# One projection of 40 rows for dt's low rank, B and C, with B and C repeated over the channels by transfers through DRAM

## The chip, the cores and the metric

The kernel runs on one core of one Trainium2 chip. The core has five engines that work side by side and meet only at semaphores: TensorE (PE in the profile; PEld is its loading of weights), VectorE (DVE), ScalarE (ACT), GpSimd (POOL) and SyncE (SP), and 16 DMA engines that all queues share. The metric is the device time of one launch in microseconds, lower is better, as a median over several runs.

## The reference, cut to what matters

Eight images of 48 x 48 tokens with 128 features pass three layers: a state space layer, a linear attention layer and a mixture of eight experts (top 2). The change lies in the first. For each token, with a 3x3 convolution `xc` of 256 channels, it computes

```python
xp = xc @ W_xproj                      # 256 -> 8 + 16 + 16
dt_r, Bp, Cp = xp[..., :8], xp[..., 8:24], xp[..., 24:]
dt  = softplus(dt_r @ W_dt + b_dt)     # 8 -> 256
dtN = dt @ W_dtN + b_dtN               # 256 -> 16
# scan over the 2304 tokens, state h of 256 channels x 16 states
h = exp(dt[:, :, None] * A) * h + (dtN * B)[:, None, :] * x[:, :, None]
y = einsum('bdn,bn->bd', h, C) + Dskip * x
```

and then a layer norm, a gate `silu(z)` and an output projection. `B` and `C` have 16 values for each token, the same for all 256 channels.

## The kernel before

An image is cut into NC = 6 chunks of T = 384 tokens. The scan puts (state n, channel j) pairs on the 128 partitions: 16 states times 8 channels make one block, so 32 blocks (NB) make a chunk, and one block is one *step*. A whole image is 192 steps, all eight images 1536. Each engine runs one long written-out program over steps k = 0 to 191 of a pass (`c, n = divmod(k, 32)`: chunk c, step n of the chunk). In one pass the scan of image i, the projections for the chunk after it, the convolution for the chunk after that, the attention of image i-1 (`w.j`, steps 22 to 125), and the experts of the two images before that (`w.p`, `w.q`; their tiles on steps 126 to 191 and 0 to 26) are interleaved by hand; the loop over passes is a pipeline of images. Nothing is scheduled at run time: an engine does its instructions in the written order and waits at each semaphore.

One step works like this. PE copies x to the 128 partitions with a small product (`spread`, L768, three PSUM banks, at most two steps ahead of the scan). DVE multiplies it in PSUM by `db_rep` (`inflow`, L1407) and scans (`scan`, L1420), with the decays that ACT has made from `dt_rep` (`decay`, L1041, three steps ahead). POOL multiplies the states by `c_rep` (`product`, L627, at most 8 steps behind), and PE sums over the states four steps at a time (`fold_quad`, L831). `dt_rep` comes from DRAM: SP stores dt once a chunk (`spread_dt`, n = 13, L487), and reads it back, repeated over the 16 states, four steps at a time (`repeat`, L501, at n = 0, 4, 8, ..., for the steps from k + 8 on). Its wait (on the scan, and three slots) holds everything behind it on SP's queue.

The projections of the chunk ahead stand in the table `SLOT` (L54) of name, step and chunk. All go through one PSUM bank, `ps_main`, in the order of the table, and each PE instruction group of them waits until the one before it has been read out:

- `dtr` at n = 0: two matmuls with 8 columns of `w_xp` (one for each half of the 256 channels), read out by ACT at n = 1 (`project`, L1093) into `dt_r`, which lies in the first 8 rows of `b_rep`.
- `dt0`, `dt1` at 3 and 7 from `dt_r`. ACT, then POOL (`rectify`, n = 11) make dt of them.
- `C` at 13 and `B` at 15: two matmuls each with `w_c`, `w_b`, which are the 16 columns repeated eight times (made once in the setup, L1337), so that the product comes out on 128 partitions. ACT reads C out at n = 14 into `c_rep` (two buffers), B at n = 16 into `b_rep`.
- `dtN` at 17, from dt with the repeated `w_n`. DVE makes `db_rep` = (dtN + bias) * `b_rep` at n = 18 (`drift`, L1446), for the next chunk.

POOL waits for C's readout before the first product of a chunk (L624), DVE at `drift` for B's (L1445). In the profile each f32 matmul is two records and two weight loads, so B and C of one chunk are eight records of 384 columns. SP's program at a step is, in order: `repeat`, `stack` (n = 2 to 7: twelve stores of parts of x into `x_stack`), `spread_dt` (13), `load_residual` (4), `store_t1` (23), loads of the next image (`load_x`), and the traffic of experts and attention.

## Time and profile before

| | |
|---|---|
| Median of 3 runs | 4248.45 us (4237.47 to 4254.57) |
| The profiled execution | 4259.8 us, its span 4257.7 us |
| PE busy | 3281.3 us, 77% |
| PE weight loads | 1995.0 us, 47% |
| DVE busy | 3117.9 us, 73% |
| POOL busy | 2942.6 us, 69% |
| ACT busy | 2565.0 us, 60% |
| Granted TensorE clock, mean | 0.890 of 2.4 GHz |
| DMA | 730.07 MB, mean 171 GB/s |
| of it SP's queue | 484.13 MB, its packets 46.5% of 16 engines' span |

An engine's busy time is a share of the whole; what binds differs from stretch to stretch. Steps run from about 80 us to 3730 us after the start. Before that lies the setup, and after it the last image's attention and experts run without a scan. A chunk takes 51 us in the first image, where only the state space layer runs, and 69 to 96 us once attention and experts run beside it.

### The profile page before, as it was taken

Reading aid. Unit: us, or ns where it says so; the run is one execution under the profiler, and the core shown is the slowest. Engines: PE = TensorE matmul, PEld = TensorE weight load, DVE = VectorE, ACT = ScalarE, POOL = GpSimd, SP = SyncE. Lnnn points to the kernel's source line nnn. Section 1 sums busy time; section 2 is a strip of 40 time slices with the busy share of each in tenths; the row PEclk is TensorE's granted clock in tenths of the full one; section 3 lists DMA queues with packets and bytes.
Section 4 is the critical chain, followed back from the end, with each engine's and each line's share of the span. In section 5 each row is a group of like instructions: output and inputs, shape, how many; then the busy total and the mean of one; then the engine's idle time right before and its main releaser. Section 6 shows DMA issues by size and latency. Waiting matters only on the chain.

```text
span 4257.7 us, 69497 instructions
## 1 busy us (share of the span) xinstructions
PE 3281.3 (77%) x17432; PEld 1995.0 (47%) x17432; DVE 3117.9 (73%) x5570; ACT 2565.0 (60%) x6151; POOL 2942.6 (69%) x2703
## 2 busy tenths in 40 slices
PE   5687887787798868987788877888688877778381
PEld 2233343343465535653465434655356534567271
DVE  3699998899867987789776988779877897723110
ACT  3465665476567656775576755676467765666151
POOL 1465675857676968679685886669686796757665
PEclk9798997898899979998899978999799988999695
DMA  4865555555787658966687676876588666868493
GB/s 103 194 154 134 145 127 124 135 144 139 189 218 201 144 142 218 235 164 145 169 226 193 146 164 177 219 195 143 140 228 233 154 149 178 221 184 231 117 257 76
DMA packets 464099, 730.07 MB, mean 171 GB/s; under 512 B 58505, under 2 KB 362194, under 8 KB 461522
## 3 DMA queue, kind: packets, MB, share of 16 engines
q1 hardware_dynamic: 313938, 484.13, 46.5%
q10 hardware_dynamic: 99072, 203.47, 16.1%
q0 software_dynamic: 50688, 37.93, 5.2%
q8 instruction: 152, 2.49, 0.3%
q14 instruction: 249, 2.04, 0.2%
HBM read 596.93 MB, written 100.07 MB: 164 GB/s over the span
## 4 chain that ended last, share of the span: by engine, by line
PE 34%; issue 17%; DVE 16%; POOL 14%; ACT 11%; DMA 4%; ACTq 2%; SPq 1%; DVEq 0%; POOLq 0%
PE ps_conv L754 7%; DVE state L1420 6%; PE ps_main L817 5%; POOL prod L627 5%; PE ps_h L921 3%; PE ps_y L831 3%; POOL rows_in L681 3%; PE ps_g L940 3%; DVE ps_x L1407 3%; PE ps_x L768 3%; PE ps_g L933 3%; POOL acc_in L709 3%; ACT dt_rep L1041 2%; ACT big_u L1169 1%; DVE silu L1661 1%
## 5 line engine op out<-in xcount | busy, mean ns | idle before, releaser
L627 POOL TENSOR_TENSOR prod<-state,c_rep 128x384 f32<-128x384 f32 x1536 | 1659.0, 1120 | 937.9 <-DVE state L1420 912.9
L1420 DVE TENSOR_TENSOR_SCAN state<-dt_rep,carry,ps_x 128x384 f32<-128x384 f32 x1280 | 1284.0, 1003 | 0.0
L1407 DVE TENSOR_TENSOR ps_x<-ps_x,db_rep 128x384 f32<-128x384 f32 x1536 | 854.0, 556 | 397.7 <-PE ps_x L768 360.0
L1041 ACT ACTIVATE dt_rep<-dt_rep,vecs 128x384 f32<-128x384 f32 x1536 | 913.3, 611 | 182.0 <-DMA dt_rep<-dt_dram 104.1
L768 PE MATMUL ps_x<-x_stack,copy 96*128 96x384 bf16 x1536 | 546.9, 357 | 392.3 <-DVE state L1420 386.4
L754 PE MATMUL ps_conv<-gx,w_conv 128*128 128x384 f32 x1728 | 695.9, 522 | 8.7 <-DVE parts L1437 6.0
L768 PEld LDWEIGHTS ps_x<-x_stack,copy 96*128 96x128 bf16 x1536 | 154.5, 101 | 882.1 <-DVE state L1420 635.9
L709 POOL DMA_INDIRECT acc_in<-rows_out,row_of x288 | 452.6, 1572 | 97.8 <-issue 46.3
L921 PE MATMUL ps_h<-u_t,w_up 128*128 128x128 f32 x2064 | 325.1, 296 | 188.4 <-DVE silu L1661 170.5
L697 POOL TENSOR_TENSOR hidden<-g_sb,silu 128x384 f32<-128x384 f32 x344 | 363.7, 1060 | 104.4 <-ACT u_out L1227 98.9
L754 PEld LDWEIGHTS ps_conv<-gx,w_conv 128*128 128x128 f32 x1728 | 320.9, 203 | 227.6 <-issue 119.7
L1221 ACT ACTIVATE g_sb<-ps_g,w_down 128x128 f32<-128x128 f32 x1032 | 304.1, 368 | 199.6 <-PE ps_g L940 164.6
L1661 DVE SCALAR_TENSOR_TENSOR silu<-silu,ps_h 128x384 f32<-128x384 f32 x344 | 185.8, 540 | 300.4 <-ACT silu L1212 193.6
L921 PEld LDWEIGHTS ps_h<-u_t,w_up 128*128 128x128 f32 x2064 | 275.5, 200 | 276.2 <-issue 165.9
L831 PE MATMUL ps_y<-prod,fold 128*32 128x384 f32 x3072 | 361.2, 545 | 22.9 <-POOL prod L627 22.9
L681 POOL DMA_INDIRECT rows_in<-big_u,row_of x288 | 291.1, 1011 | 83.8 <-issue 76.4
L940 PE MATMUL ps_g<-w_down,hidden 128*128 128x128 f32 x2064 | 299.4, 282 | 34.1 <-POOL hidden L697 25.4
L933 PE MATMUL ps_g<-u_t,w_up 128*128 128x128 f32 x2064 | 309.4, 288 | 11.9 <-ACT u_out L1227 8.1
L933 PEld LDWEIGHTS ps_g<-u_t,w_up 128*128 128x128 f32 x2064 | 289.3, 202 | 51.4 <-issue 25.9
L940 PEld LDWEIGHTS ps_g<-w_down,hidden 128*128 128x128 f32 x2064 | 268.2, 198 | 41.7 <-POOL hidden L697 29.0
L1420 DVE TENSOR_TENSOR_SCAN state<-dt_rep,ps_x 128x384 f32<-128x384 f32 x256 | 241.4, 943 | 16.4 <-ACT carry L1050 16.4
L1212 ACT ACTIVATE silu<-ps_h 128x384 f32<-128x384 f32 x344 | 168.1, 489 | 48.6 <-POOL hidden L697 38.6
(245 smaller groups left out, 4928.9 us busy)
## 6 DMA issues: line engine op xcount, KB each, us to landing
dt_rep<-dt_dram SPq DMA_DIRECT2D x384, 768.0 KB
w_up<-in_w_exp ACTq DMA_DIRECT2D x344, 384.0 KB
w_down<-in_w_exp ACTq DMA_DIRECT2D x344, 193.5 KB
x_stack<-parts SPq DMA_DIRECT2D x576, 48.0 KB
u_in<-rows_in SPq DMA_DIRECT2D x344, 64.5 KB
rows_out<-u_out SPq DMA_DIRECT2D x344, 64.0 KB
dt_dram<-dt SPq DMA_DIRECT2D x192, 96.0 KB
x_in<-in_x SPq DMA_DIRECT2D x48, 192.0 KB
```

Source lines behind the costliest of these rows:

```text
L627: pool.tensor_tensor(prod[:, k % HS, :], state[:, k % HS, :], c_rep[:, c % 2, :], ALU.mult).then_inc(s_prod.sem, 1)
L681: pool.indirect_dma_start(rows_in, bass.IndirectOffsetOnAxis(ap=row_of[:, parity(m), k:k + 1], axis=0), big_u[:, k % NT, :], None).then_in ...
L709: pool.indirect_dma_start(acc_in[:, x % GA], None, rows_out, bass.IndirectOffsetOnAxis(ap=row_of[:, parity(m), n * NT + x:n * NT + x + 1], ...
L754: ins = pe.matmul(aux(use)[:, 0:T], w_conv[:, tap, P * hf:P * hf + P], gx[:, ROWS * c + dy:ROWS * c + dy + ROWS, dx:dx + W], start=tap == ...
L768: pe.matmul(ps_x[k % XB][:, 0:T], copy[:, b, :], x_stack[:, c % 2, HV * q + hf, :], start=True, stop=True).then_inc(s_xrep.sem, 1)
L831: ins = pe.matmul(ps_y[32 * q:32 * q + 32, 0:T], fold[:, b, :], prod[:, (QD * m + q) % HS, :], start=b == 0, stop=b == 3)
L921: ins = pe.matmul(aux(name)[:, P * k:P * k + P], w_up[:, u % WA, P * k:P * k + P], u_t[:, u % UT, :], start=True, stop=True)
L933: ins = pe.matmul(aux(name)[:, P * k:P * k + P], w_up[:, u % WA, F + P * k:F + P * k + P], u_t[:, u % UT, :], start=True, stop=True)
L940: ins = pe.matmul(aux(name)[:, F:F + P], hidden[:, v % HID, P * k:P * k + P], w_down[:, v % WB, P * k:P * k + P], start=k == 0, stop=k == ...
L1041: act.activation(dt_rep[:, g % XS, q, :], dt_rep[:, g % XS, q, :], ACT.Exp, scale=decay_rate).then_inc(s_decay.sem, 1)
L1407: dve.tensor_tensor(x_n, x_n, db_rep[:, c % 2, :], ALU.mult).then_inc(s_inflow.sem, 1)
L1420: dve.tensor_tensor_scan(state[:, k % HS, :], dt_rep[:, g % XS, q, :], ps_x[k % XB][:, 0:T], init, ALU.mult, ALU.add).then_inc(s_state.sem, 1)
```

## The change

`dtr`, `B` and `C` become one use `xp` of the bank, at n = 0: two matmuls with all 40 columns of `w_xp`. ACT reads its 40 rows out at n = 1 into a new tile `xp` [40, 384]; the two products `dt0` and `dt1` read its first 8 rows. The two uses `C` and `B` on PE, their readouts on ACT and the tiles `w_b`, `w_c` are gone (and with them four small copies of the setup). In their place SP stores rows 8 to 40 of `xp` to DRAM at n = 2 (32 rows of 1536 bytes, 48 KB) and at n = 9 reads them back twice, 16 rows repeated eight times each, into `b_rep` and `c_rep` (192 KB each). New waits: SP at n = 2 for `xp`'s readout and the transfers of the chunk before; SP at n = 9 for the store, the last `drift` and the products of an earlier chunk; ACT before it reads out `xp`, for the last store; POOL at n = 0 and DVE at `drift` for both transfers.

```diff
-SLOT = (("dtr", 0, 1), ("dt0", 3, 1), ("mean", 5, -1), ("dt1", 7, 1), ("var", 9, -1), ("C", 13, 1), ("B", 15, 1),
-        ("dtN", 17, 1), ("out", 19, -1), ("z0", 23, 2), ("z1", 26, 2))
+SLOT = (("xp", 0, 1), ("dt0", 3, 1), ("mean", 5, -1), ("dt1", 7, 1), ("var", 9, -1), ("dtN", 17, 1), ("out", 19, -1), ("z0", 23, 2), ("z1", 26, 2))
...
-        dt_r = b_rep[0:RK, :]
+        xp = sb("xp", [RK + 2 * NS, T])
...
+            def spread_bc(w, c, n):
+
+                i, cc = w.cell(c + 1)
+                if i is None:
+                    return
+                if n == 2:
+                    sp.wait_ge(*read(i, f"xp{cc}"))
+                    apart()
+                    before_it, bc = w.cell(c - 1)
+                    due(sp, s_bc, before_it, bc + 1)
+                    sp.dma_start(bc_dram[cc % 2], xp[RK:RK + 2 * NS, :]).then_inc(s_bcdram.sem, 16)
+                else:
+                    due(sp, s_bcdram, i, cc + 1)
+                    apart()
+                    before_it, bc = w.cell(c)
+                    if before_it is not None:
+                        sp.wait_ge(*read(before_it, f"dtN{bc}"))
+                    apart()
+                    old, oc = w.cell(c - 1)
+                    due(sp, s_prod, old, NB * (oc + 1))
+                    for k, dst in enumerate((b_rep[:, :], c_rep[:, cc % 2, :])):
+                        rows = bc_dram[cc % 2, NS * k:NS * k + NS, :].unsqueeze(1).broadcast_to([NS, JB, T])
+                        sp.dma_start(dst, rows).then_inc(s_bc.sem, 16)
...
                     if n == 13:
                         spread_dt(w, c)
+                    if n in (2, 9):
+                        spread_bc(w, c, n)
...
                 if n == 0:
-                    pool.wait_ge(*read(i, f"C{c}"))
+                    due(pool, s_bc, i, c + 1)
...
-                    if name == "dtr":
+                    if name == "xp":
                         pe.wait_ge(*read(i, f"conv1{cc}"))
-                        lhs, rhs, rows = w_xp[:, :, 0:RK], xc[:, cc % 3], RK
-                    elif name == "B":
-                        lhs, rhs, rows = w_b, xc[:, cc % 3], P
-                    elif name == "C":
-                        lhs, rhs, rows = w_c, xc[:, cc % 3], P
+                        lhs, rhs, rows = w_xp, xc[:, cc % 3], RK + 2 * NS
...
-                if n == STEP["dtr"] + 1:
+                if n == STEP["xp"] + 1:
                     if before_it is not None:
-                        act.wait_ge(*read(before_it, f"dtN{bc}"))
-                    evacuate(i, f"dtr{cc}", dt_r[:, :], aux(f"dtr{cc}")[0:RK, 0:T])
+                        due(act, s_bcdram, before_it, bc + 1)
+                    evacuate(i, f"xp{cc}", xp[:, :], aux(f"xp{cc}")[0:RK + 2 * NS, 0:T])
...
-                if n == STEP["C"] + 1:
-                    old, oc = w.cell(c - 2)
-                    due(act, s_prod, old, NB * (oc + 1))
-                    evacuate(i, f"C{cc}", c_rep[:, cc % 2, :], aux(f"C{cc}")[:, 0:T])
-                if n == STEP["B"] + 1:
-                    if before_it is not None:
-                        act.wait_ge(*read(before_it, f"dtN{bc}"))
-                    evacuate(i, f"B{cc}", b_rep[:, :], aux(f"B{cc}")[:, 0:T])
...
-                dve.wait_ge(*read(i, f"B{cc}"))
+                due(dve, s_bc, i, cc + 1)
```

## Rows read from the trace of the kernel before

**Rows 1.** Stretches: start:end, us, busy PE, PEld, DVE, ACT, POOL; clock, DMA share, GB/s

```profile
1518.00:1608.00 90.00, 66.02 (x270) 35.53 (x270) 74.01 (x178) 44.50 (x103) 54.43 (x49) 0.80 0.62 148
1608.00:1703.00 95.00, 78.15 (x487) 55.77 (x486) 68.53 (x113) 63.15 (x165) 80.19 (x81) 0.96 0.83 225
1703.00:1787.00 84.00, 74.72 (x484) 51.92 (x483) 61.91 (x97) 59.42 (x158) 55.31 (x55) 1.00 0.90 230
1787.00:1864.00 77.00, 66.75 (x382) 41.98 (x381) 59.53 (x102) 59.81 (x149) 45.93 (x45) 0.93 0.76 200
1864.00:1933.00 69.00, 62.18 (x331) 38.01 (x329) 60.46 (x85) 49.88 (x101) 60.68 (x49) 0.95 0.60 130
1933.00:2007.00 74.00, 54.67 (x237) 26.82 (x237) 69.04 (x124) 43.41 (x97) 71.39 (x64) 0.82 0.67 153
...
80.00:175.00 95.00, 51.99 (x168) 19.18 (x167) 52.95 (x83) 34.25 (x71) 35.68 (x35) 0.73 1.02 215
175.00:520.00 345.00, 279.42 (x1162) 117.21 (x1161) 331.26 (x522) 209.62 (x434) 218.19 (x210) 0.91 0.61 146
```

**Rows 2.** The page's chain that ended last, by engine

```profile
PE 34%; issue 17%; DVE 16%; POOL 14%; ACT 11%; DMA 4%; ACTq 2%; SPq 1%; DVEq 0%; POOLq 0%
```

**Rows 3.** DVE's waits, us, times, longest: 1518 to 2007, then 520 to 1000

```profile
DVE ps_x L1407 <- PE ps_x L768: 54.9, 58, 3.5
...
DVE ps_x L1407 <- PE ps_x L768: 27.1, 36, 4.0
```

**Rows 4.** The same from 1547, 1646, 1731.7, 1817, 1889.6, some 13 us each

```profile
DVE ps_x L1407 <- PE ps_x L768: 5.6, 2, 3.5
...
DVE ps_x L1407 <- PE ps_x L768: 1.8, 2, 1.0
...
DVE ps_x L1407 <- PE ps_x L768: 1.2, 1, 1.2
...
DVE ps_x L1407 <- PE ps_x L768: 5.3, 3, 3.1
...
DVE ps_x L1407 <- PE ps_x L768: 1.3, 2, 0.9
```

**Rows 5.** Groups by line and shape: busy us, mean ns | idle before

```profile
L817 PE MATMUL ps_main<-xc,w_c 128*128 128x384 f32 x192 | 85.4, 574 | 5.6 <-DVE y L1482 5.6
L817 PE MATMUL ps_main<-xc,w_b 128*128 128x384 f32 x192 | 80.6, 547 | 3.6 <-ACT c_rep L1032 3.6
...
L831 PEld LDWEIGHTS ps_y<-prod,fold 128*32 128x32 f32 x3072 | 62.7, 112 | 119.6 <-issue 68.6 <-POOL prod L627 38.4
...
L1032 ACT ACTIVATE c_rep<-ps_main 128x384 f32<-128x384 f32 x48 | 23.8, 495 | 13.8 <-PE ps_main L817 13.3 <-POOL prod L627 0.5
L1032 ACT ACTIVATE b_rep<-ps_main 128x384 f32<-128x384 f32 x48 | 23.6, 492 | 69.6 <-PE ps_main L817 66.6 <-issue 3.0
...
L817 PEld LDWEIGHTS ps_main<-xc,w_xp 128*8 128x8 f32 x192 | 15.7, 101 | 54.0 <-issue 51.2 <-DVE sz L1457 2.2
```

**Rows 6.** Chain of work in order of time: start, us, what (B's four records)

```profile
1554.73 2.76 PE ps_main L817 x4
...
2141.58 1.29 PE ps_main L817 x4
```

**Rows 7.** Timeline of ACT, SP and DVE between 2006 and 2053 us

```profile
2006.65 0.48 ACT L1032 ACTIVATE b_rep<-ps_main 8x384 f32<-8x384 f32 x1 [3.01 <-PE ps_main L817]
...
2007.08 3.51 SPq L478 DMA_DIRECT2D x_stack<-parts  x4
...
2023.49 0.57 SPq L501 DMA_DIRECT2D dt_rep<-dt_dram  x1
...
2052.99 0.59 DVE L1446 SCALAR_TENSOR_TENSOR db_rep<-ps_main,vecs,b_rep 128x384 f32<-128x384 f32 x1
```

**Rows 8.** Chain of work, 2090 to 2116 us

```profile
2097.83 0.39 SPq L511
...
2103.32 12.34 DMA x_in<-in_x
```

More of the change, by code:

```diff
@@ L38 @@
 SC = NB * NC
-N_CLEAR, N_SETUP = 3, 17
+N_CLEAR, N_SETUP = 3, 13
 GROUPS = NC * NB // QD
@@ L167, in build @@
         w_xp = sb("w_xp", [P, HV, RK + 2 * NS])
-        w_b, w_c, w_n = (sb(n, [P, HV, P]) for n in ("w_b", "w_c", "w_n"))
+        w_n = sb("w_n", [P, HV, P])
         w_dtn = sb("w_dtn", [P, HV, NS])
@@ L365, in build @@
         s_dtdram = Sem("s_dtdram", NC, 16 * QD)
+        s_bcdram, s_bc = Sem("s_bcdram", NC, 16), Sem("s_bc", NC, 32)
         s_rep = [Sem(f"s_rep{b}", GROUPS // XS, 16) for b in range(XS)]
@@ L402, in build @@
         dt_dram = nc.dram_tensor("dt_dram", [2, HV, 32, QD * T], F32, kind="Internal").ap()
+        bc_dram = nc.dram_tensor("bc_dram", [2, 2 * NS, T], F32, kind="Internal").ap()
         t1_dram = nc.dram_tensor("t1_dram", [B, P, NT * D], F32, kind="Internal").ap()
@@ L783, in main @@
                     hf = int(name[-1])
-                    pe.wait_ge(*read(i, f"dtr{cc}"))
-                    ins = pe.matmul(o[:, 0:T], w_dt[:, P * hf:P * hf + P], dt_r[:, :], start=True, stop=True)
+                    pe.wait_ge(*read(i, f"xp{cc}"))
+                    ins = pe.matmul(o[:, 0:T], w_dt[:, P * hf:P * hf + P], xp[0:RK, :], start=True, stop=True)
                 elif name in ("z0", "z1"):
@@ L1333, in _ @@
             dve.wait_ge(s_const.sem, n_const)
-            for k, (dst, src) in enumerate(((w_b, w_xp[:, :, RK:RK + NS]), (w_c, w_xp[:, :, RK + NS:RK + 2 * NS]), (w_n, w_dtn[:, :, :]))):
+            for k, (dst, src) in enumerate(((w_n, w_dtn[:, :, :]),)):
                 for hf in range(HV):
```

## The prediction

> **What bounds the kernel now.** I read the table of stretches first, cut at the readout of `dtr`, so that each row is one chunk of one image [rows 1]. No engine is the bound all along. The first image alone (175 to 520 us) is DVE's: 331 of 345 us busy. In an image with everything running (1518 to 2007 us) the chunks differ: in the third to fifth PE is busy 75 of 84, 67 of 77 and 62 of 69 us; in the second (80 of 95 us) and the sixth (71 of 74 us) POOL is; in the first nobody is, but PE runs at a granted clock of 0.80 there, so for a good part of it at 1.2 instead of 2.4 GHz. The page's chain says the same from another side: PE has 34% of it, DVE 16, POOL 14, ACT 11 [rows 2]. So work taken from PE is worth something, at less than its full price.
>
> How much less is read where the work stands. PE and DVE are tied step by step: PE may be two steps ahead of the scan, no more. When C at n = 13 and B at n = 15 push PE back, DVE shows an idle time before L1407, put down to PE's L768. In the image from 1518 to 2007 us DVE waits so for 54.9 us in all, in the 480 us from 520 only 27.1 [rows 3]. I asked for the same wait from C's start to some 5 us behind B in each of the six chunks: 5.6, 1.8, 1.2, 5.3, 1.3 and, with no row, nothing in the sixth [rows 4].
>
> **The change part by part.**
>
> *PE.* Eight matmul records a chunk go, 166.0 us busy in all 48 chunks (85.4 and 80.6) [rows 5]. In the chain B's four records count 1.29 us at the full clock and 2.76 at half of it [rows 6]. What DVE gets back in a chunk is the smaller of its idle time and of what is removed. In the first chunk of an image both C (full clock) and B (half) could give 4.05 us, in the fourth (C at half) about 3.7; the others are under the cap. Sum for an image: 4.05 + 1.8 + 1.2 + 3.7 + 1.3 + 0 = 12.05 us. Five images run like this (1000 to 3490 us): 60 us. For the image from 520 I take half, 6 us; for the first one 1 us, since DVE is 96% busy; for the two chunks behind 3490 us 5 us. That is 72 us. I then take off the second chunk of each of the five (9 us), because POOL is the bound there and sets its own pace, and a quarter of the remaining 63: PE that comes earlier meets other waits, on DVE's expert work or POOL, which these idle times don't count. That quarter is a judgement. Kept: 48 us. The bounds are 0 (another path is as late everywhere) and 166 us (all of it on the path); 72 is the row-based value before deductions.
>
> *Weight loads.* `xp` loads 40 columns where `dtr` loaded 8. A load of 8 takes 101 ns, one of 32 takes 112 [rows 5], so 192 loads cost 2 us of PE's own queue, beside running matmuls. Nothing.
>
> *ACT.* Two readouts a chunk of 495 and 492 ns go, 47 us busy, and with them 79.9 us of waiting for PE [rows 5]. ACT carries 11% of the chain. The readout of `xp` has 40 rows instead of 8, which doesn't matter: its length is in the columns. I count 0, between 0 and a gain of 11% of 47, 5 us.
>
> *The wait of SP at n = 2.* SP now stands until ACT has read `xp` out; behind it are the rest of `stack`, `repeat` at n = 4 and all loads. It isn't late: the readout begins at 2006.65 us and lasts 0.48, and SP's first `stack` of n = 2, which itself had to wait for PE's L768 of the same step, begins at 2007.08, with two issues before the new wait [rows 7]. The wait is satisfied when reached. ACT's new wait, for the store of the chunk before, is 31 steps old. Cost 0, up to 0.5 us a chunk.
>
> *The store and the two loads.* Three issues on SP, 0.4 to 0.6 us each as L511 and L501 [rows 7, 8]: SP is on the path in one place that I found. At the start of an image's second chunk the chain runs through SP's issues into `x_in<-in_x` (12.34 us) and on to PE [rows 8]. `load_x` at n = 2 now has the store ahead of it: 0.5 us, six times, 3 us.
>
> *Arrival.* The loads go out at n = 9, right behind `repeat` of n = 8, which is at 2023.49 us; `drift` needs `b_rep` at 2052.99 [rows 7]. That leaves 29 us. The slowest landing near by is the 192 KB of `x_in`, 12.34 us [rows 8]; a plain 384 KB at the 230 GB/s of a full stretch [rows 1] is 1.7 us. In the first image the chunk is 51 us instead of 89, so I scale 29 to 17 us: still more than 12.34. POOL needs `c_rep` later still. The store has seven steps (17 us here, 10 there) to land before n = 9. So both DRAM hops are hidden. What can't be hidden is where the queues are full: from 80 to 175 us their busy share is 1.02 at 215 GB/s [rows 1], since DRAM is cleared then. 0.43 MB (48 + 384 KB) for each of two chunks is 2 us each: 4 us. The bound is 14 us, if `drift` waits there for one more landing like the one of 12.34.
>
> *The clock.* The chunks in which PE is busy 73 or 74% of the time (first and sixth) have a granted clock of 0.80 and 0.82; those with 82 to 90% have 0.93 to 1.00 [rows 1]. Less PE work may mean more time at 1.2 GHz. PE's share falls by about 2 points of 100, and 15 points go with 0.15 of clock, so perhaps 0.02. If the rise in PE's time has the same share on the path as B and C have (12 of 166 / 8 = 21 us an image), 0.02 of 0.9 on 400 us is 9 us of PE and 5 of the path, 25 us for five images. But PE is less busy in those chunks also because it waits for others, and the work removed stands where PE is late. I count 7 us, bounds 0 and 40. The Trainium skill's page "TensorE: Matmul & The Clock Gate" (section "What's actually happening") has the direction of this: the throttled clock is the default and activity releases it. The trace's chunks agree in that order; no run yet shows it for a removal.
>
> The skill's page "DMA: Bandwidth & Descriptors" (section "Measured") speaks against such small transfers: it calls those under 64 KB descriptor-dominated and asks for 1 MiB. The store has 48 KB. No row here shows a lone 48 KB store; the rule can hold in full and still cost nothing where there is slack.
>
> *The sum.* 48 - 3 - 4 - 7 = 34 us. The profiled execution is at 4259.8 us, 11.3 over the median of the three runs, so I take the difference over: 4225.8 there, 4248.45 - 34 = **4214 us** as the median.
>
> **The rivals.**
>
> *Same: the gain is taken back.* Either the clock (40 us instead of 7, the bound above) or the paths beside PE. For it: DVE 61 to 74 us and POOL 46 to 80 us busy in each chunk, three engines within 20% of each other. Against it: the idle times of [rows 4] follow the removed groups directly. 48 - 7 - 40 = 1 us: 4247 us.
>
> *Slower: SP's queue.* SP writes every `dt_rep` load, and these have little to spare. If at n = 9 the store hasn't landed, SP stands, and with it the `repeat` of n = 12, itself behind 384 KB more. Price where it bites: 1.7 us of transfer and about as much of waiting, 3.3 us. It would bite where the queues are fullest (second and third chunk, shares 0.83 and 0.90 [rows 1], twelve chunks) and in the six short chunks of the first image: 18 x 3.3 = 59 us. Gain kept elsewhere 34. 34 - 7 - 59 = -32: 4280 us. It decides once the store takes over some 10 us in the first image or 17 later; against it, nothing near by of that size takes so long.
>
> *More gain.* All 72 us and ACT's 5 are kept and the clock doesn't move: 77 - 7 = 70, so 4178 us. If the coupling gives still more, up to half the 166 us net, 4165.
>
> *The change doesn't do what it says:* the projections are surely gone from PE; nothing else does their work. No case of its own.
>
> **How the numbers follow.** A difference under 0.5% (21 us) can't be told from none for this kernel. Forecast, a gain of 21 to 60 us: 0.52. More gain: 0.10. Same: 0.22, around 4247. Slower, around 4280: 0.16. So faster 0.62, same 0.22, slower 0.16. The range takes in forecast, the greater gain down to 4165, and the same case up to 4268 (0.5% over the median before), so that beside the greater part of the slower rival little is left out; the forecast's own range is 4188 to 4227.
>
> **What the profile after would show.** PE's busy time lower by about 160 us with the two groups of 192 records gone, ACT's by 47; DVE's wait for L768 in an image down from 54.9 to 43 or so, the third to fifth chunks shorter by 1 to 4 us each, the sixth unchanged, the first image unchanged. Step wrong signs: a wait of DVE L1446 or POOL L627 on a transfer of `b_rep` or `c_rep` in steady chunks (arrival); ACT's L1041 waiting longer for `dt_rep` than before (SP's queue); a mean clock under 0.87 (clock). The forecast is wrong, too, if chunks stay as long with DVE's idle time moved to another place: then another path was as late.

## The result and the profile after

The changed kernel is slower: 4272.83 us as the median of six runs (4266.86 to 4288.71), against 4249.1 us for the kernel before on the same chip, ratio 1.0045 with an interval of 1.0024 to 1.0066. By the ratio that is 19 us, less than the 0.5% that the prediction called too little to tell, but the interval leaves out 1. The forecast was 34 us faster. The profiled execution after is the fastest of its six, 4266.86 us with a span of 4265.0; that before is above its median. So the two profiles are only 7 us apart, and below I go by chunks and by ratios, not by the two spans.

The page of the changed kernel, its busy times, its chain by engine and two of its groups (busy us, mean ns, idle before and its releaser):

```profile
PE 3220.9 (76%) x17048; PEld 1959.0 (46%) x17048; DVE 3125.1 (73%) x5566; ACT 2523.2 (59%) x6055; POOL 2938.9 (69%) x2703
...
PE 30%; DVE 19%; issue 19%; POOL 16%; ACT 10%; DMA 3%; ACTq 2%; SPq 1%; DVEq 0%; POOLq 0%
...
L1422 DVE TENSOR_TENSOR ps_x<-ps_x,db_rep 128x384 f32<-128x384 f32 x1536 | 854.2, 556 | 377.8 <-PE ps_x L795 351.2
...
L795 PE MATMUL ps_x<-x_stack,copy 96*128 96x384 bf16 x1536 | 558.9, 365 | 428.0 <-DVE state L1435 423.8
```

ACT lost 42 us as it should. PE lost 60.4 us and not the 166 of [rows 5]: 106 us of its time came back. It came back in groups that nobody touched, with as many records as before: the folds are busy 20.4 us longer, the convolution 17.4, the product of `w_n` 13.7, the copies of x 12.0. The product of `w_n` takes 585 ns where it took 506, and the wait of `drift` for it is 35.1 us where it was 20.4. The same 192 records with `xp` cost what they cost with `dtr` (645 against 648 ns). Groups by shape, changed kernel:

```profile
L840 PE MATMUL ps_main<-xc,w_xp 128*40 128x384 f32 x192 | 97.5, 645 | 4.7 <-DVE parts L1452 2.8 <-DVE sz L1472 1.8
L840 PE MATMUL ps_main<-dt,w_n 128*128 128x384 f32 x192 | 87.1, 585 | 0.0
...
L1461 DVE SCALAR_TENSOR_TENSOR db_rep<-ps_main,vecs,b_rep 128x384 f32<-128x384 f32 x48 | 29.3, 610 | 35.2 <-PE ps_main L840 35.1
...
L1055 ACT ACTIVATE xp<-ps_main 40x384 f32<-40x384 f32 x48 | 23.1, 482 | 71.2 <-PE ps_main L840 71.2
L840 PEld LDWEIGHTS ps_main<-xc,w_xp 128*40 128x40 f32 x192 | 23.0, 143 | 48.6 <-issue 45.9 <-DVE sz L1472 2.2
```

The mean granted clock is 0.870, before it was 0.890. With two levels, 1.0 and 0.5, a stretch of length L at a mean of c has spent 2(1 - c)L at 1.2 GHz: 936 us of the whole before, 1105 after.

From here a chunk is the 32 steps from one scan's first step to the next chunk's, written image.chunk (0.2 is the third chunk of the first image). The first to sixth stretch of [rows 1] are chunks 3, 4, 5 and then 0, 1, 2 of the next image. *Light* chunks are 0.1, 0.2, 0.3, 0.5, 1.0 and 2.0, where few other layers run beside the scan. Times in us, in brackets those at 1.2 GHz; for images 3 to 6 the mean of the four:

| | six light chunks | chunk 0 | 1 | 2 | 3 | 4 | 5 |
|---|---|---|---|---|---|---|---|
| before | 319.1 (56) | 81.9 | 71.3 | 73.1 | 87.1 | 94.7 (9.3) | 84.5 |
| after | 332.9 (125) | 77.3 | 71.6 | 73.0 | 86.5 | 97.5 (11.4) | 83.8 |
| e1 | 332.5 (121) | 78.3 | 71.3 | 73.2 | 86.0 | 99.3 (18.5) | 83.7 |
| e2 | 324.5 (79) | 80.7 | 70.8 | 73.1 | 85.6 | 95.5 (9.9) | 83.7 |
| e3 | 316.8 (23) | 78.3 | 71.9 | 73.1 | 86.8 | 97.9 (14.2) | 83.9 |
| e13 | 334.0 (126) | 77.9 | 71.4 | 73.1 | 86.0 | 95.2 (7.4) | 84.4 |
| e17 | 323.2 (33) | 77.4 | 71.8 | 73.3 | 85.6 | 94.6 (9.2) | 84.6 |

The loss is in two places: 14 us in the six light chunks, and 2.7 us (unrounded) in chunk 4 of each late image, which takes back most of the 4.6 us that chunk 0 gains. A chunk of one profile is one sample. Chunk 4 takes 97.6 to 99.3 us in the other kernels that have it as the changed one has (e1, e3, e9, e10), and 95.4 to 95.7 in those with C and B, or work of their size, in it (e2, e7, e12, e16). Both places are read next.

**The light chunks.** Chunk 0.2, by stretch (us, busy PE, PEld, DVE, ACT, POOL, clock, DMA share, GB/s), first before, then after:

```profile
223.27:274.89 51.62, 42.34 (x179) 16.91 (x178) 51.14 (x80) 31.34 (x64) 35.35 (x35) 0.93 0.62 150
```

```profile
227.20:281.59 54.39, 44.12 (x171) 17.45 (x170) 51.50 (x80) 30.51 (x62) 35.32 (x35) 0.81 0.64 150
```

Eight records fewer, and PE is busy 1.8 us longer. PE's timeline at n = 15 to 18 of this chunk (start, us, what, idle before it), before:

```profile
247.06 1.46 PE L817 MATMUL ps_main<-xc,w_b 128*128 128x384 f32 x4
248.35 0.33 PE L768 MATMUL ps_x<-x_stack,copy 96*128 96x384 bf16 x1
248.70 1.56 PE L754 MATMUL ps_conv<-gx,w_conv 128*128 128x384 f32 x4
250.10 0.33 PE L768 MATMUL ps_x<-x_stack,copy 96*128 96x384 bf16 x1
250.26 1.46 PE L817 MATMUL ps_main<-dt,w_n 128*128 128x384 f32 x4
```

The same place after, first PE, then the two places where DVE waits for it:

```profile
247.63 0.34 PE L795 MATMUL ps_x<-x_stack,copy 96*128 96x384 bf16 x1 [1.03 <-DVE state L1435]
249.86 0.50 PE L795 MATMUL ps_x<-x_stack,copy 96*128 96x384 bf16 x1 [1.90 <-DVE state L1435]
250.29 1.51 PE L854 MATMUL ps_y<-prod,fold 128*32 128x384 f32 x8
...
253.51 2.92 PE L781 MATMUL ps_conv<-gx,w_conv 128*128 128x384 f32 x4
256.23 0.53 PE L795 MATMUL ps_x<-x_stack,copy 96*128 96x384 bf16 x1
256.55 2.38 PE L840 MATMUL ps_main<-dt,w_n 128*128 128x384 f32 x4
...
256.79 0.57 DVE L1422 TENSOR_TENSOR ps_x<-ps_x,db_rep 128x384 f32<-128x384 f32 x1 [0.58 <-PE ps_x L795]
258.97 0.62 DVE L1461 SCALAR_TENSOR_TENSOR db_rep<-ps_main,vecs,b_rep 128x384 f32<-128x384 f32 x1 [0.70 <-PE ps_main L840]
```

Where C and B stood, PE idles for 1.03 and 1.90 us with one copy of x between. From 249.86 everything takes nearly twice its time: the convolution 2.92 instead of 1.56 us. A DVE that is busy 51 of 52 us now stands twice for PE (1.3 us, and 0.3 in a third wait at n = 20). That the time lost is on DVE's own path is why so small a delay counts in full.

This is the greater part of the chunk's 2.8 us, not all. DVE also waits at the start of the chunk, 1.3 us in two waits where it was 0.5 us in one:

```profile
230.58 0.57 DVE L1422 TENSOR_TENSOR ps_x<-ps_x,db_rep 128x384 f32<-128x384 f32 x1 [1.01 <-PE ps_x L795]
```

That wait stands in a stretch at 1.2 GHz which both kernels have: it begins at n = 28 of the chunk ahead and lasts 10.2 us here, 6.8 before the change. Why it is longer isn't shown.

**Chunk 4 of the late images.** The four steps from n = 14 to 18 of chunk 4.4, before, then after:

```profile
2136.49:2146.50 10.01, 9.81 (x63) 6.89 (x61) 8.24 (x13) 8.19 (x21) 8.36 (x9) 0.98 0.86 231
```

```profile
2154.34:2166.37 12.03, 9.13 (x54) 6.30 (x54) 9.57 (x14) 7.45 (x18) 9.75 (x11) 0.86 0.79 210
```

And the timeline there after the change, PE, then DVE:

```profile
2153.59 0.32 PE L795 MATMUL ps_x<-x_stack,copy 96*128 96x384 bf16 x1
2156.03 1.45 PE L944 MATMUL ps_h<-u_t,w_up 128*128 128x128 f32 x6 [2.12 <-DVE silu L1676]
2157.27 0.42 PE L933 MATMUL ps_h<-eye,u_in 128*128 128x128 f32 x1
2157.62 1.51 PE L854 MATMUL ps_y<-prod,fold 128*32 128x384 f32 x8
2159.06 0.50 PE L795 MATMUL ps_x<-x_stack,copy 96*128 96x384 bf16 x1
...
2159.60 0.57 DVE L1422 TENSOR_TENSOR ps_x<-ps_x,db_rep 128x384 f32<-128x384 f32 x1 [2.42 <-PE ps_x L795]
...
2162.83 1.61 DVE L1407 SCALAR_TENSOR_TENSOR gmv<-gmv 128x1 f32<-128x1 f32 x1
```

PE waits 2.12 us for `silu` where C used to run, and then the experts' product takes 1.45 us (0.83 to 0.93 at full clock), the fold 1.51 (0.85). DVE waits 2.42 us for the copy of x behind them. In the clock records of the changed kernel and of e1, e3, e6 and e9 a stretch at 1.2 GHz touches the scan's step n = 15 in each of the chunks 2.4 to 5.4. In those of the kernel before, e2, e5 and e7 none does; most have theirs one to three steps earlier.

The 2.02 us between 10.01 and 12.03 overstate the clock's part. 1.5 us of them are `gmv`, a DVE instruction that takes 1.61 us here and in 5.4, and 0.13 in 3.4 and 6.4, where the four steps take 10.28 us; why is not shown. The ten steps from n = 14 to 24 are a better measure, since the steps ahead of n = 14 vary by some microseconds within each kernel. Before, they take 28.0 us in each of the chunks 3.4 to 6.4. After, they take 29.5, 31.6, 31.7 and 29.6.

**Chunk 1 of the late images.** Chunk 4.1 gains 1.5 us by n = 19 and has lost it again at n = 30. DVE's sum over q stands behind ACT's exp and that behind POOL's subtraction. Before, POOL and then DVE:

```profile
1921.02 2.74 POOL L649 TENSOR_TENSOR qv<-qv,q_max 128x1152 f32<-128x1152 f32 x1
...
1924.99 2.55 DVE L1615 TENSOR_REDUCE q_sum<-qv 128x144 f32<-128x2304 f32 x1 [1.11 <-ACT qv L1254]
```

After:

```profile
1940.41 2.73 POOL L676 TENSOR_TENSOR qv<-qv,q_max 128x1152 f32<-128x1152 f32 x1
...
1944.38 2.55 DVE L1630 TENSOR_REDUCE q_sum<-qv 128x144 f32<-128x2304 f32 x1 [3.18 <-ACT qv L1269]
```

POOL and `q_sum` stand 19.39 us later than before, DVE's scan ahead of them only 17.32 us: the scan came earlier, POOL did not, and DVE waits the difference. Over the eight images the wait is 20.4 us, where it was 9.2:

```profile
L1630 DVE TENSOR_REDUCE q_sum<-qv 128x144 f32<-128x2304 f32 x8 | 20.4, 2553 | 20.4 <-ACT qv L1269 20.4
```

**The places of [rows 4].** The same steps after, in the same order, DVE's waits for the copy of x (us, times, longest; no row in the sixth again):

```profile
DVE ps_x L1422 <- PE ps_x L795: 4.0, 3, 2.1
...
DVE ps_x L1422 <- PE ps_x L795: 2.1, 1, 2.1
...
DVE ps_x L1422 <- PE ps_x L795: 1.6, 3, 1.0
...
DVE ps_x L1422 <- PE ps_x L795: 1.8, 2, 1.2
...
DVE ps_x L1422 <- PE ps_x L795: 0.4, 1, 0.4
```

9.9 us instead of 15.2: the waits didn't vanish with C and B, only the fourth and fifth fell clearly.

### The profile page after: what moved, and what is told of

The parts are those of the page before. It is cut to its first block, busy times and chain, and to the rows that moved or that the text cites. A ratio compares the mean times of both kernels' runs of the same rounds, so it can differ in the third digit from the quotient of the medians.

```text
span 4265.0 us, 68846 instructions
## 1 busy us (share of the span) xinstructions
PE 3220.9 (76%) x17048; PEld 1959.0 (46%) x17048; DVE 3125.1 (73%) x5566; ACT 2523.2 (59%) x6055; POOL 2938.9 (69%) x2703
## 3 DMA queue, kind: packets, MB, share of 16 engines
q1 hardware_dynamic: 330066, 505.37, 48.1%
q10 hardware_dynamic: 99072, 203.47, 16.1%
q8 instruction: 149, 2.44, 0.2%
## 4 chain that ended last, share of the span: by engine, by line
PE 30%; DVE 19%; issue 19%; POOL 16%; ACT 10%; DMA 3%; ACTq 2%; SPq 1%; DVEq 0%; POOLq 0%
DVE state L1435 7%; PE ps_conv L781 6%; POOL prod L654 6%; PE ps_main L840 4%; DVE ps_x L1422 3%; PE ps_h L944 3%; POOL rows_in L708 3%; POOL acc_in L736 3%; PE ps_y L854 3%; PE ps_g L956 3%; PE ps_g L963 3%; PE ps_x L795 2%; ACT dt_rep L1064 2%; POOL hidden L724 1%; ACT big_u L1184 1%
## 5 line engine op out<-in xcount | busy, mean ns | idle before, releaser
L795 PE MATMUL ps_x<-x_stack,copy 96*128 96x384 bf16 x1536 | 558.9, 365 | 428.0 <-DVE state L1435 423.8
L781 PE MATMUL ps_conv<-gx,w_conv 128*128 128x384 f32 x1728 | 713.3, 533 | 14.3 <-DVE parts L1452 11.4
L854 PE MATMUL ps_y<-prod,fold 128*32 128x384 f32 x3072 | 381.6, 573 | 25.4 <-POOL prod L654 24.9
L708 POOL DMA_INDIRECT rows_in<-big_u,row_of x288 | 289.1, 1004 | 83.8 <-issue 73.9
```

Source lines behind the costliest of these rows:

```text
L708: pool.indirect_dma_start(rows_in, bass.IndirectOffsetOnAxis(ap=row_of[:, parity(m), k:k + 1], axis=0), big_u[:, k % NT, :], None).then_in ...
L781: ins = pe.matmul(aux(use)[:, 0:T], w_conv[:, tap, P * hf:P * hf + P], gx[:, ROWS * c + dy:ROWS * c + dy + ROWS, dx:dx + W], start=tap == ...
L795: pe.matmul(ps_x[k % XB][:, 0:T], copy[:, b, :], x_stack[:, c % 2, HV * q + hf, :], start=True, stop=True).then_inc(s_xrep.sem, 1)
L854: ins = pe.matmul(ps_y[32 * q:32 * q + 32, 0:T], fold[:, b, :], prod[:, (QD * m + q) % HS, :], start=b == 0, stop=b == 3)
```

## The experiments

Each product called small is 128x128x128 in f32 into the bank that the next copy of x overwrites, so nobody reads it. Ratios are to the kernel before on the same chip. Of two kernels that ran on different chips, the ratios differ clear of noise if they are about 0.003 apart (12 us), an estimate from their intervals.

**e1: are the transfers the cause?** The changed kernel without them and the waits on them.

```diff
-                    if n in (2, 9):
-                        spread_bc(w, c, n)
...
-                    due(pool, s_bc, i, c + 1)
...
-                due(dve, s_bc, i, cc + 1)
```

> The changed kernel without its store and two loads a chunk and without the waits for them; b_rep and c_rep hold 0.5 from the setup on, so B and C are constants and the output is another. PE, ACT, DVE and POOL do what they do in the changed kernel. Clock theory (taking C and B from PE leaves a hole at n = 13 to 17 in which TensorE falls to 1.2 GHz, and what PE does then sets DVE back): stays at or a few us under the changed kernel, 4260 to 4272 us, the chunks of the first image still 54.4 us long and at 1.2 GHz for some 20 us of each. Rival (the transfers on SP's queue and the DMA engines eat the gain): 4215 to 4240 us, first image's chunks 51.4 us or less.

Measured: 4268.84 us, ratio 1.0034 (1.0012 to 1.0055), clock 0.868. The light chunks take 332.5 us as after the change, chunk 4 no less. The slowdown is there without a single added transfer. What the transfers cost is the 0.1% between 1.0034 and 1.0045; the intervals don't part it from nothing, and allow up to 0.4%.

**e2: put PE's work back, keep the transfers.** Two products of C's and B's size at n = 13 and 15.

```diff
+                    if n in (13, 15):
+                        fill(w, c)
```

> The changed kernel with two products of C's and B's size put back on PE at n = 13 and 15 (four records each, w_out by xc, into ps_main, which dtN overwrites; nobody reads them). Readouts on ACT stay gone, transfers stay. Clock theory: more PE work, yet faster: the first image's chunks are back at 51.4 us, nine such chunks give back 26 us, the late images lose the 3 us an image at n = 12 of their first chunk that the change had won; sum 4245 to 4260 us. Rival (transfers): the time of the changed kernel plus what C and B cost, 4275 to 4300 us.

Measured: 4259.99 us, 1.0021 (1.0001 to 1.0040), clock 0.883. More work for PE and no more time, by the middles 10 us less, which the intervals don't part from nothing. The chunks tell more; chunk 0.2:

```profile
220.60:272.44 51.84, 42.56 (x179) 17.11 (x178) 51.14 (x80) 30.64 (x62) 35.32 (x35) 0.93 0.66 157
```

It is back at 51.8 us and chunk 4 at 95.5, but chunk 0 of the late images goes from 77.3 back to 80.7: the real gain of the change is given up as well.

**e3: the clock alone, early.** Three small products ahead of the copies of x at n = 12 to 16 and 28 to 31 in images 0 and 1.

```diff
+                for _ in range(extra):
+                    pe.matmul(ps_x[k % XB][:, 0:P], eye[:, :], full_ones[:, :], start=True, stop=True)
```

> The changed kernel with three small f32 products (128x128 by 128 columns, unread, into the bank that the same step's copy of x fills next) ahead of the copy of x at n = 12 to 16 and n = 28 to 31, in the passes that scan images 0 and 1 only. Clock theory: PE stays at 2.4 GHz there, nine chunks lose their 3 us each: 4240 to 4250 us, and the time at 1.2 GHz in a chunk of the first image falls from 20 to under 7 us. Rival (transfers, or PE's work itself): 4273 us or more.

Measured: 4256.7 us, 1.0013 (0.9999 to 1.0028). Chunk 0.2 never leaves the full clock and is a little shorter than before the change:

```profile
221.65:273.04 51.39, 44.35 (x226) 21.60 (x225) 51.13 (x81) 30.59 (x62) 35.38 (x35) 1.00 0.65 159
```

The light chunks lose 16.1 us against the change (332.9 to 316.8), the median 14 by the ratios. C and B are still gone and the transfers still there: the clock by itself is the loss in the light chunks. (e3 gives some back in image 1, where chunk 5 takes 58.2 instead of 53.7 us.)

**e7: the same products in the kernel before,** as the control.

> The kernel before with the early warming products of e3_warm_early. Clock theory: C and B already keep PE at 2.4 GHz at n = 13 to 17, only the 7 us at n = 28 of each early chunk are left and DVE is the bound there: 0 to 8 us under the kernel before. Rival (the warming gives by itself, whatever the change did): 15 us or more under the kernel before.

Measured: 4267.69 us, 1.0032 (1.0015 to 1.0048), clock 0.899. Where C and B fill the gap already, the products bring nothing and cost 0.3%.

**e4: e3 and two small products at steps 83 to 125 of every image,** where the records show the most time at 1.2 GHz.

```diff
-                    spread(w, k + XB - 1, 3 if isinstance(w.i, int) and w.i <= 1 and n in (12, 13, 14, 15, 16, 28, 29, 30, 31) else 0)
+                    spread(w, k + XB - 1, 3 if isinstance(w.i, int) and w.i <= 1 and n in (12, 13, 14, 15, 16, 28, 29, 30, 31) else 2 if 83 <= k < 126 else 0)
```

> As the last, and two such products also at steps 83 to 125 of every image, where TensorE is at 1.2 GHz for 44 to 50 of 87 us and then for 24 to 27 of 94 us in both kernels. Clock theory: PE is late there because of its clock, so 2 to 6 us an image more, 4215 to 4235 us. Rival: PE's low clock there only fills waiting time, and extra work costs: 4250 us or more.

Measured: 4278.2 us, 1.0064 (1.0042 to 1.0085), clock 0.891. The mean clock is as high as before the change and the time is worse; chunk 3 takes 90.2 instead of 86.8 us (in a profile 18 us above the median of its runs). The mean clock doesn't tell what a kernel loses by it; the place does.

**e9, e10: only where the light chunks have the hole.** Two small products at n = 12 to 16 of the six light chunks (e9), and three more at n = 28 to 31 of the first four chunks of image 0 (e10).

> The changed kernel with two warming products ahead of the copy of x at n = 12 to 16 only, and only in the six chunks in which the change lengthened the scan and an earlier warming shortened it (chunks 1, 2, 3, 5 of image 0, chunk 0 of images 1 and 2). Clock theory (it is the hole where C and B stood): these chunks return to 51.4 to 55 us each, 3 us each, 18 us under the changed kernel: 4248 to 4258 us. Rival (the hole is not it; e3 gained by its other products at n = 28 to 31): 4265 us or more.

> As the last, and three products at n = 28 to 31 of the first four chunks of image 0, where both kernels fall to 1.2 GHz for 7 us. If PE's clock matters there too: 1 to 4 us under e9_warm_narrow. Rival (DVE is the bound there at either clock): within 2 us of it, or slower for the work added.

Measured: 1.0014 (1.0000 to 1.0028) and 1.0010 (0.9993 to 1.0028). Both end where e3 does by their ratios. In e9 the light chunks take 326.7 us, 6 of the 14 back: DVE's waits behind n = 9 are gone in 0.1, 0.3 and 0.5 (1.3 to 1.6 us each after the change), those at the chunk's start are not. In 0.2, which still takes 54.7 us, two products don't hold the clock. e10 has 324.7. So the hole of C and B is about half of what the light chunks lose, and the longer stretch at n = 28 belongs to the rest.

**e5, e6: does POOL take the gain of the late images?** POOL relieved in the kernel before (e5) and in e3 (e6): its product `hidden` has 32 of 384 columns in steps 128 to 159, q's subtraction and multiplication 8 groups.

```diff
-                    pool.tensor_tensor(hidden[:, u % HID, :], g_sb[:, u % 2, :], silu[:, u % 2, :], ALU.mult).then_inc(s_hidden.sem, 1)
+                    cols = 32 if 320 <= t < 352 else F
+                    pool.tensor_tensor(hidden[:, u % HID, 0:cols], g_sb[:, u % 2, 0:cols], silu[:, u % 2, 0:cols], ALU.mult).then_inc(s_hidden.sem, 1)
```

> The kernel before with POOL relieved: the product hidden of an expert tile has 32 of its 384 columns in the chunk in which the rows are scattered (steps 128 to 159), and the subtraction and the multiplication of q by its maximum and its sum cover 8 of 72 and 8 of 48 groups; the output is another. That takes some 25 us of POOL's work out of each late image. POOL theory (in the late images POOL, busy 80 of 95 and 71 of 74 us, sets the pace, and what PE gains is lost again in front of it): 5 to 20 us an image less, 4150 to 4220 us. Rival (the late images are set by the whole loop of PE, ACT and DVE, POOL no more than others): under 3 us an image, 4240 us or more.

> The same relief in the changed kernel with the early warming products of e3_warm_early (the output is another). POOL theory: with POOL out of the way the late images keep what the change gives, so this is faster than e5_before_relief by more than e3_warm_early was against the kernel before (which was slower by 0.13%): by 10 us or more, 3 us an image at least. Rival (PE's gain is lost to something else): within 5 us of e5_before_relief, or slower.

Measured: 4219.71 us, 0.9938 (0.9916 to 0.9959), and 4202.44 us, 0.9896 (0.9869 to 0.9923). With POOL relieved the change with the early products is worth 17 us (4219.71 to 4202.44); without, e3 was at or above the kernel before. In images 3 to 6 the change takes 21 us off (1947.0 to 1925.5). Without relief it takes 4 off by e3 (1971.1 to 1967.5), but 12 by the changed kernel's own profile, which has the same code there (1958.8), and e9 and e10 spread as far (1957.4, 1969.6); so that comparison is coarse. By chunk, e5 to e6: chunk 1 from 70.1 to 68.5 us, where it did not fall unrelieved (71.3 and 71.1 in the kernel before and e7, 71.3 to 71.9 in the changed kernel, e1, e3, e9 and e10); chunk 3 from 87.1 to 85.3, little more than it varies between kernels that are alike there (87.1 before, 85.5 in e7); chunk 5 the other way, 82.4 to 84.3. So POOL's part is real and stands mainly at q's subtraction in chunk 1: about 1.6 us an image. It isn't the whole answer to the late images: chunk 4, where the relief of `hidden` was, went from 94.4 to 95.1, not down.

**e8, e11, e12: can POOL's work go to DVE?** e8 is e3 with `hidden` of steps 128 to 159 on DVE; e11 is e9, e12 the kernel before, both with q's subtraction on DVE.

```diff
-                        due(pool, s_qmax, m, 1)
-                        pool.tensor_tensor(q_heads[:, n * h:n * h + n], q_heads[:, n * h:n * h + n],
...
+                        due(dve, s_qmax, m, 1)
+                        dve.tensor_tensor(q_heads[:, n * h:n * h + n], q_heads[:, n * h:n * h + n],
```

> The changed kernel with the early warming products, and with the product hidden of the tiles of steps 128 to 159 moved from POOL to DVE, one step later (some 0.55 us on DVE instead of 1.06 on POOL, 16 tiles an image; the output stays). POOL theory: that chunk (97 us) loses 5 to 12 us, 4190 to 4230 us. Rival: DVE waits in order for the tiles and the scan behind it is late: 4260 us or more.

> e9_warm_narrow with the subtraction of the maximum from q (steps 56 and 57 of every image) on DVE instead of POOL, the output stays. POOL's part of that is 5.2 us an image in a chunk where POOL is busy 71 of 74 us. POOL theory: the chunk goes from 73 to about 71 us, and what PE gains one chunk earlier is kept: 3 us an image, 4220 to 4235 us. Rival (DVE's own 2.4 us more in that chunk cost what POOL saves): 4245 us or more.

> The kernel before with the same subtraction on DVE. POOL theory: 1 to 2 us an image from POOL alone, 4230 to 4245 us, and so slower than e11_warm_qsub_dve by 5 us or more. Rival: no more than e11 gains over e9, equal to e11_warm_qsub_dve within 4 us, so that the change has no part in it.

Measured: 1.0000 (0.9981 to 1.0019), 1.0071 (1.0048 to 1.0094) and 1.0073 (1.0044 to 1.0103). e8 can't be told from e3, and its chunk 4 is longer, 100.0 instead of 97.9 us. With the subtraction on DVE chunk 1 takes 75.1 and 75.0 us instead of 71.4 and 71.3, with and without the change: DVE pays 3.7 us for what POOL's lateness costs 1.6. POOL is late there, DVE is not free there.

**e13: is chunk 4 the clock too?** Only the changed kernel and three small products at n = 12 to 14 of chunk 4.

```diff
+                    spread(w, k + XB - 1, 3 if k // NB == 4 and n in (12, 13, 14) else 0)
```

> The changed kernel with three products of 128x128x128 (f32, into the bank that the next copy of x overwrites) ahead of the copy of x at steps n = 12, 13 and 14 of the fifth chunk of every image's scan (the second stretch of rows 1), nothing else. Chunks 3.4 to 6.4 take 94.7 us on average before and 97.5 after the change; in every kernel without C and B there is a stretch of 3.4 us at 1.2 GHz at n = 14 in that chunk, in no kernel with them. Theory (the give-back in the late images is the clock too): that stretch goes, these chunks are 2 to 3 us shorter than after the change, the step from n = 15 to 16 takes 2.4 instead of 3.9 us, and the whole is 8 to 15 us under the changed kernel, ratio to before 1.001 to 1.003. Rival (POOL or a transfer sets the chunk's pace, the clock is a companion): chunks stay at 97 us or more, ratio 1.004 to 1.006.

Measured: 4253.99 us, 1.0004 (0.9988 to 1.0020), 17 us under the changed kernel. Steps n = 14 to 18 of chunk 4.4:

```profile
2149.32:2158.38 9.06, 7.02 (x55) 5.32 (x53) 8.07 (x14) 7.09 (x17) 7.32 (x8) 1.00 0.87 244
```

12.03 us have become 9.06, at the full clock, and that is 0.95 us under the kernel before: this is what C and B were worth here. The ten steps from n = 14 to 24 take 27.2 us in each of the chunks 3.4 to 6.4 (28.0 before, 29.5 to 31.7 after). The step from n = 15 to 16 of chunk 4 takes 2.44 us in images 3 to 6; it took 2.27 to 2.44 before the change and 3.44 to 3.92 after it. POOL has the same work in all three (79.4, 78.9 and 79.0 us busy in chunk 4.4 before, after and in e13). The rival, that POOL or a transfer sets the pace there, falls.

**e16: C and B put back in chunk 4 only.**

```diff
+                    if c == 4 and n in (13, 15):
+                        fill(w, c)
```

> The changed kernel with two products of C's and B's size (their result unread) at n = 13 and 15 of the fifth chunk of the scan only. This puts PE's work of before back where the late images lose. Theory of the clock: chunks 3.4 to 6.4 at 94 to 96 us, no 1.2 GHz stretch at n = 14, ratio 1.001 to 1.003. Rival: 97 us or more, ratio 1.0045 or above, since PE's work there is only dearer.

Measured: 4257.34 us, 1.0008 (0.9995 to 1.0020). The same four steps:

```profile
2155.15:2165.17 10.02, 9.95 (x63) 6.89 (x61) 8.25 (x14) 7.90 (x20) 7.93 (x9) 0.97 0.84 219
```

10.02 us, within a hundredth what they took before, and the ten steps to n = 24 take 28.0 again in all four images. Putting PE's work back in one chunk of six takes 16 us off the program by the ratios, and `gmv` is short again.

**e14, e15: real work in the hole.** `dtN` at n = 14 instead of 17, alone and with e13's products.

```diff
-SLOT = (("xp", 0, 1), ("dt0", 3, 1), ("mean", 5, -1), ("dt1", 7, 1), ("var", 9, -1), ("dtN", 17, 1), ("out", 19, -1), ("z0", 23, 2), ("z1", 26, 2))
+SLOT = (("xp", 0, 1), ("dt0", 3, 1), ("mean", 5, -1), ("dt1", 7, 1), ("var", 9, -1), ("dtN", 14, 1), ("out", 19, -1), ("z0", 23, 2), ("z1", 26, 2))
```

> The changed kernel with dtN at n = 14 instead of 17 (and so drift at 15 instead of 18): real work of four records stands in the gap that C and B left, no work is added. POOL's dt is done some 1.2 us before n = 14 in the light chunks, 2 us after it in the sixth stretch. Theory of the clock: in the light chunks of image 0 the additional stretch at 1.2 GHz at n = 13 to 16 is shorter or gone, chunks 0.1 to 0.3 and 0.5 near 52 instead of 53.7 to 55.2 us; whole 8 to 20 us under the changed kernel, ratio 1.000 to 1.0025. Rival (the gap only moves to n = 17, where conv stands alone): light chunks stay at 54 us, ratio 1.004 to 1.005; and where PE stands waiting for POOL's dt ahead of the copies of x, late chunks get longer by a microsecond each, ratio over 1.005.

> Both: dtN at n = 14, and the products of e13 in the fifth chunk. If both holes in PE's work cost through the clock, the two gains add: 15 to 30 us under the changed kernel, ratio 0.997 to 1.001. If the late chunks go by another path, as e14 alone.

Measured: 4293.07 us, 1.0102 (1.0081 to 1.0123), and 4280.98 us, 1.0061 (1.0042 to 1.0079). The theory missed, and the rival has only the sign: the light chunks improve by 1.2 us of 333, and of the late chunks mainly chunk 4 grows, to 99.9 us (chunk 0 to 79.5). e15 is 17 us under e14, but its profile, 22 us above its median, has chunk 4 at 100.2 and doesn't show where. In 0.2 `dtN` still comes behind an idle time and runs at half the clock; in chunk 4.4 its four records stand ahead of the copy of x that DVE needs, and `drift` waits:

```profile
244.34 0.34 PE L795 MATMUL ps_x<-x_stack,copy 96*128 96x384 bf16 x1 [1.90 <-DVE state L1435]
244.61 0.85 PE L854 MATMUL ps_y<-prod,fold 128*32 128x384 f32 x8
245.39 2.93 PE L840 MATMUL ps_main<-dt,w_n 128*128 128x384 f32 x4
...
2172.28 0.62 DVE L1461 SCALAR_TENSOR_TENSOR db_rep<-ps_main,vecs,b_rep 128x384 f32<-128x384 f32 x1 [2.27 <-PE ps_main L840]
```

A hole has to be filled from where it begins, and with work that nobody waits for.

**e17, e18: both holes closed, and the control.** Three small products at n = 12 to 14 of chunk 4 and at n = 12 to 16 and 28 to 31 of the six light chunks, in the changed kernel (e17) and in the kernel before (e18).

> The changed kernel with three products of 128x128x128 ahead of the copy of x where runs so far showed that the hole costs: at n = 12 to 14 of the fifth chunk of every image, and at n = 12 to 16 and 28 to 31 of the six light chunks (0.1, 0.2, 0.3, 0.5, 1.0, 2.0), and nowhere else. Theory (two separate places where the clock took the gain): e13's 17 us and some 14 to 16 us of the light chunks add, 30 us under the changed kernel, ratio to before 0.996 to 0.9985; light chunks together 316 to 320 us, fifth chunks 94 to 96 us. Rival (a microsecond gained early only moves which chunk meets which transfer, and the gains don't add): ratio 0.9995 to 1.0015.

> The kernel before with the same products in the same places. Theory (in the fifth chunk C and B themselves keep the clock up; what is left to gain there is nothing, in the light chunks 2 us): same as before, ratio 0.999 to 1.003, so that the change under equal conditions is worth 10 to 25 us. Rival (the products would bring the same 30 us to either kernel, so the loss of the change isn't the hole that C and B left): ratio 0.992 to 0.995.

Measured: e17 4237.40 us, 0.9966 (0.9951 to 0.9980), e18 4262.54 us, 1.0025 (1.0010 to 1.0040). The two gains add (17 and 14 us alone, 34 together, from 1.0045 to 0.9966), though not as cleanly as expected: the light chunks end at 323 us and not at 316 to 320 (0.1 and 0.5, behind chunks without products, keep over 9 us at 1.2 GHz and take 54.6 and 54.5 us). By the intervals the 34 can be 23 to 45 (an estimate). The products slow the kernel before by 10.6 us; in its profile the light chunks grow to 332 us and chunk 4 to 97.0. They speed the changed one up by 34. e17 is 14 us faster than the kernel before.

## Why the prediction was wrong

*The clock* is the term that failed: 7 us counted, 34 us measured (the changed kernel to e17), and more if the products themselves cost something. If that cost is f, between 0 and the 10.6 us that e18 shows, the clock took 34 to 45 us, and the change without it is worth 14 + f, 14 to 25 us. That is an estimate: it holds if the products of e17 close all that the change opened, and if they gain nothing at n = 28 to 31 that the kernel before lost as well (e10 against e9: 2 us in the light chunks). The difference is the loss of 19 to 20 us that was measured. The bound of 40 us, which stood in the rival *Same*, was about the value. Three steps led past it. First, I sized the effect by a mean, "15 points go with 0.15 of clock, so perhaps 0.02". The mean fell by just that 0.02 (0.890 to 0.870, so that even the sign named for the clock, a mean under 0.87, stayed away), and it doesn't give the price: e4 has 0.891 and is the slowest of the first experiments. Second, I looked for it in the five full images and took "the first image unchanged" since DVE is 96% busy there. But a chunk that DVE fills is one where PE has gaps, and where each delay of PE's answer lands on DVE: +2.8 us in 0.2. Third, I wrote that "the work removed stands where PE is late". In chunk 4 this is true one step later; at n = 13 itself PE waits for `silu`, and C kept it busy meanwhile.

The Trainium skill's page "TensorE: Matmul & The Clock Gate" warns of this under "HAM oscillation — how this bites in real kernels": waits inside a loop throttle the array, and the following matmuls start slow each time round. Its case waits for DMA. Here the trace agrees behind a removal: 1.03 and 1.90 us of idle, and then the convolution at 2.92 instead of 1.56 us in chunk 0.2.

*The kept gain of 48 us* was too high as well. Without the clock's loss the change is worth 14 to 25 us, and 41 were on the list (48 - 3 - 4; a quarter off 63 leaves 47.25, so 48 is rounded up). The cap by DVE's idle time held in one stretch: the fourth, 3.7 us promised, 4.6 measured (81.9 to 77.3; 3.1 without chunk 5.0, which is long before for a reason that isn't known). By [rows 6] C at half the clock and B at full are 4.05 us there, not 3.7. In the first, 4.05 were promised and 0.6 came; in 3.3 and 4.3 the records show 13.7 us at 1.2 GHz around n = 14 to 17, where it was 10.2. In the fifth the 1.3 us came and was given back within the chunk, at POOL's subtraction: the "other waits, on DVE's expert work or POOL" for which a quarter was taken off. They took nearly all of it there. In the second I had taken the gain out because "POOL is the bound there"; e13 shows that POOL isn't the bound where C and B stood, since 17 us come from PE's clock in that chunk alone. DVE's wait for the copies of x in an image was to fall from 54.9 to 43 us. It is

```profile
DVE ps_x L1422 <- PE ps_x L795: 56.6, 58, 6.3
```

in the same 192 steps after [rows 3]. That was the named sign of "another path was as late", and it came true.

*The transfers, SP and ACT* went as written, within what can be told. Neither the transfer of `b_rep` nor that of `c_rep` releases a wait of DVE or POOL. SP's waits come to 6.7 us in the whole run at n = 9 and to 1.0 at n = 2 (first and second row); an issue of the store takes 0.62 us (third):

```profile
SPq L512 <- POOL prod L654: 6.7, 16, 1.0
...
SPq L458 <- ACT xp L1055: 1.0, 2, 0.9
...
2028.63 0.62 SPq L500 DMA_DIRECT2D bc_dram<-xp x1
```

`load_x` in chunk 4.4 is issued 6.5 us after the chunk's start where it was 5.85, so the later issue that was priced at 0.5 us is real. *Slower: SP's queue* was right in sign and wrong in cause; e1 has no store and is as slow. Its sum takes the clock's 7 us off 34, from which they were gone already; without that it would have said 4273, and that this is the measured time is chance. The start of the first scan moved from 85.95 to 90.03 us, but e1 without transfers starts at 93.09: the 4 us for full queues are not shown.

*Weight loads*: 143 ns for 40 columns, not 112, so 7 us more of loading (15.7 to 23.0) where 2 were counted, beside running matmuls still. *ACT*: -42 us busy, 0 on the path.

What stays open: why chunk 5.0 takes 85 to 89 us in the profiles of the kernel before, e5, e7, e12 and e18, and 78 to 85 without C and B, when chunks 3.0, 4.0 and 6.0 differ by 3 us; why the light chunks of e18 take 332 us and those of e7, with the same products in most of them, 318.6, so that f isn't known better than from 0 to 10.6 us; why the stretch at 1.2 GHz at n = 28 is longer after the change; why `gmv` takes 1.61 us; and what share of the 0.1% between e1 and the changed kernel is the transfers'.

## What to carry to other kernels

Here work removed from TensorE was a gain only where the gap it left was filled: before cutting a product out, look at what PE does just before and behind it, and at who waits for the products behind. Price the clock by place (which products would run at half speed, and who stands for them), not by a mean over the run. Where the gap can't be closed by moving work, a few small unread products in the right steps can be worth more than they cost (34 us here), and the same products elsewhere only cost (10.6 us in the kernel before).

## What the runs showed of the hardware

- Less work kept PE busy for longer: in chunk 0.2, 171 records took 44.1 us busy where 179 took 42.3, at a granted clock of 0.81 against 0.93.
- A gap of 1.03 and 1.90 us with one bf16 copy of 0.34 us between was followed by 1.2 GHz; with three f32 products of 128 columns a step there and at n = 28 to 31 (e3) the clock stayed at 2.4 GHz through the whole chunk (1.00).
- A weight load of 40 columns takes 143 ns, between the 101 of 8 columns [rows 5] and the 202 of 128 (`w_n` before the change).
- 2 x 48 transfers that repeat 16 rows over 128 partitions, 192 KB each, and 48 stores of 48 KB cost 0.1% of the time, which isn't told from nothing (up to 0.4% by the intervals), with the queue of SP's transfers at 48.1% instead of 46.5%.
